# State-space stage: GpSimd takes four of sixteen C products, in-place products in a ring of four states, separate B and C rings

## The reference, cut to what matters

```python
x = einsum('ed,bld->bel', in_proj_w, ctx)            # 512 channels, 512 positions, 4 batches
u = silu(conv(x, conv_w) + conv_b)                   # 4 taps
x_dbl = einsum('ke,bel->bkl', x_proj_w, u)           # dt_lo (16), B (16), C (16)
delta = softplus(dt_proj_w @ dt_lo + dt_proj_b);  A = -exp(A_log)
def step(state, (d_t, B_t, C_t, u_t)):
    state = state * exp(d_t[..., None] * A) + (d_t * u_t)[..., None] * B_t[:, None, :]
    return state, einsum('ben,bn->be', state, C_t)
y = (ys + D * u) * silu(z)                           # z = layernorm(x)
```

## Time and profile before

| what | us |
|---|---|
| median of 3 runs | 2925.61 (2925.49 to 2928.29) |
| profiled execution, span from first to last instruction | 2923.8 |
| the runs' median over that span (what lies around it) | 1.8 |
| VectorE scans L689, 128 | 292.7 |
| VectorE products with C L698, 128 | 180.7 |
| GpSimd input products L624, 128 | 300.9 |

### The profile page before, as it was taken

How to read it: one execution, slowest core, us unless ns; L and a number is a source line. 1 busy time by engine, 2 the same in 40 slices (tenths; PEclk the granted TensorE clock), 3 DMA queues, 4 the chain that set the end, 5 groups by cost and what they waited for, 6 DMA issues and landing times. The chain is left out here.

```text
span 2923.8 us, 42347 instructions
## 1 busy us (share of the span) xinstructions
PE 2490.2 (85%) x11348; PEld 1764.4 (60%) x11366; DVE 1863.9 (64%) x3083; ACT 1281.9 (44%) x2516; POOL 1538.0 (53%) x1262
## 2 busy tenths in 40 slices
PE   5998986597218699999999983999999999999797
PEld 2333432275216577777777762778777777877553
DVE  6999999865206544664444445775776676565586
ACT  4566664242106532322222211555555555555375
POOL 2656556323660166677666726774664665444122
PEclk8999999888659899999999995999999999999999
DMA  6989898635553499998778746443543543343101
GB/s 201 291 273 295 260 294 280 209 116 222 198 198 115 178 327 321 324 318 288 256 255 267 251 140 193 156 155 124 162 154 110 174 155 119 101 130 101 58 1 58
DMA packets 271499, 572.10 MB, mean 196 GB/s; under 512 B 26992, under 2 KB 92656, under 8 KB 270592
## 3 DMA queue, kind: packets, MB, share of 16 engines
q1 hardware_dynamic: 218080, 381.54, 39.6%
q0 software_dynamic: 44032, 167.80, 17.1%
q10 hardware_dynamic: 9248, 21.11, 2.1%
HBM read 361.69 MB, written 208.67 MB: 195 GB/s over the span
## 5 line engine op out<-in xcount | busy, mean ns | idle before, releaser
L624 POOL TENSOR_TENSOR b_u<-du,bc 128x1024 f32<-128x1024 f32 x128 | 300.9, 2351 | 214.7 <-DVE c_state L698 103.7
L450 PE MATMUL ps_y<-c_state,ident 128*128 128x512 f32 x512 | 255.1, 625 | 90.2 <-DVE c_state L698 90.2
L2002 ACT ACTIVATE prob<-ps_s,neg,q_rs 128x512 f32<-128x512 f32 x256 | 196.9, 773 | 264.1 <-DVE neg L2192 256.6
L689 DVE TENSOR_TENSOR_SCAN state<-ps_decay,b_u 128x1024 f32<-128x1024 f32 x128 | 292.7, 2287 | 14.6 <-POOL b_u L624 2.3
L1519 PE MATMUL ps_o<-w_dn,hid_t 96*128 x632 | 297.8, 593 | 0.0
L1555 ACT ACTIVATE silu_g<-ps_gu 128x192 f32<-128x192 f32 x159 | 52.5, 330 | 531.5 <-PE ps_gu L1500 531.5
L2096 POOL TENSOR_SCALAR prob<-prob,rden 128x512 f32<-128x512 f32 x256 | 174.6, 691 | 199.6 <-DVE rden L2200 199.6
L1500 PE MATMUL ps_gu<-w_gu_high,rows_t_high 128*128 (+1 forms) x636 | 228.2, 359 | 12.2 <-POOL w_gu_low L1385 10.8
L450 PEld LDWEIGHTS ps_y<-c_state,ident 128*128 128x128 f32 x512 | 92.8, 194 | 234.5 <-DVE c_state L698 143.9
L1385 POOL TENSOR_TENSOR w_gu_low<-raw_gu,w_gu_high 128x1536 fp32r<-128x1536 f32 x64 | 223.5, 3492 | 11.7 <-POOL w_gu_high L1383 11.7
L522 ACT ACTIVATE ps_decay<-delta,a_neg 128x511 f32<-128x511 f32 x256 | 165.7, 681 | 140.9 <-DVE state L689 139.7
(11 more groups left out here) (349 smaller groups left out, 6054.8 us busy)
## 6 DMA issues: line engine op xcount, KB each, us to landing
bc<-bc_dram SPq DMA_DIRECT2D x128, 512.0 KB
raw_gu<-in_gate_up POOLq DMA_DIRECT2D x64, 768.0 KB, 5.7
rows<-rows_dram SPq DMA_DIRECT2D x160, 256.0 KB, 4.7
y_dram<-y SPq DMA_DIRECT2D x158, 256.0 KB, 4.5
rows_dram<-zeros SPq DMA_DIRECT2D x46, 768.0 KB
w_q<-wq_dram SPq DMA_DIRECT2D x64, 512.0 KB, 3.6
w_o<-wo_dram SPq DMA_DIRECT2D x16, 2048.0 KB
w_dn<-in_down POOLq DMA_DIRECT2D x64, 384.0 KB, 6.1
```

Source lines behind the costliest of these rows:

```text
L450: mm = pe.matmul(ps_y[e][:, :], c.ident[:, :], c_state[:, q % 2, g, :], start=False, stop=False)
L624: pool.tensor_tensor(out=b_u[:, q % 2, :, :], in0=slot(du, n).rearrange("p (a l) -> p a l", a=1).broadcast_to([P, G, SEQ]), in1=bc[:, g % ...
L689: dve.tensor_tensor_scan(state[:, q % 2, :], decay[q % 2][:, :], b_u[:, q % 2, :, :].rearrange("p g l -> p (g l)"), 0.0, ALU.mult, ALU.add ...
L2002: act.activation(prob[:, qt, :], ps_s[qt % 2][:, :], ACT.Exp, scale=q_rs[:, k % 2, qt:qt + 1], bias=neg[:, qt:qt + 1], accum_out=den[:, qt ...
```

## The change

The product with C of the steps q with q % 16 in (1, 5, 9, 13) goes from VectorE to GpSimd, which makes `help_product(q-3)` ahead of `input_product(q)`. The products, helped or not, are made in place in `state`, now a ring of four; `c_state` is gone. `b_u` is a ring of three, and the input product no longer waits for product(q-3) and waits for scan(q-3) instead of scan(q-2). B and C rows have rings and semaphores of their own (three and four groups). `load_b(g)` waits for the input products of group g-3, `load_c(g)` for the products of group g-4. TensorE adds a helped step one step later. The context has one buffer, loaded once the projections that read it are done. The two zero-filled buffers are 194 tiles, of which 194 and 66 are filled.

```diff
-FILLS, FILL, FILL_Y = BATCH * NG // 2 - 1, 14, 5
...
-        BR = 3
+        B_RING, C_RING, U_RING, S_RING = 3, 4, 3, 4
+        HELPED = (1, 5, 9, 13)
...
-        ctx_t = p.sb("ctx_t", [P, 2, KC, SEQ])
+        ctx_t = p.sb("ctx_t", [P, KC, SEQ])
...
+        def helped(q):
+            return q >= 0 and q % PAIR in HELPED
+        def by_pool(q):
+            return sum(map(helped, range(q)))
+        def by_vector(q):
+            return max(q, 0) - by_pool(q)
...
             def load_ctx(b):
+                wait(sp, x_made, b * EC)
...
-                wait(sp, product_made, 2 * (g - BR + 1))
...
+            def load_b(g):
+                wait(sp, input_made, 2 * (g - B_RING + 1))
...
+            def load_c(g):
+                wait(sp, product_made, by_vector(2 * (g - C_RING + 1)))
+                wait(sp, help_made, by_pool(2 * (g - C_RING + 1)))
...
-                load_bc(g)
+                load_b(g)
+                load_c(g)
                 if r == 4 and b + 2 < BATCH:
-                    sp.wait_ge(x_made, (b + 1) * EC)
                     load_ctx(b + 2)
...
-                for dram, skip, n in ((m.rows_dram, 0, FILLS * FILL), (m.y_dram, MINT, FILLS * FILL_Y)):
+                for dram, skip, n in ((m.rows_dram, 0, MAXT + 2), (m.y_dram, MINT, MAXT + 2 - MINT)):
...
+            def add_up(q):
+                for g in range(G):
+                    mm = pe.matmul(ps_y[q % 2][:, :], c.ident[:, :], rows_of(state, q)[:, g, :], start=False, stop=False)
+                return mm
...
-                pe.wait_ge(product_made, q + 1)
-                for g in range(G):
-                    mm = pe.matmul(ps_y[e][:, :], c.ident[:, :], c_state[:, q % 2, g, :], start=False, stop=False)
-                mm.then_inc(product_used, 1)
+                if helped(q - 1):
+                    pe.wait_ge(help_made, by_pool(q))
+                    add_up(q - 1).then_inc(help_used, 1)
+                if not helped(q):
+                    pe.wait_ge(product_made, by_vector(q + 1))
+                    add_up(q).then_inc(product_used, 1)
...
-                waits(bc_loaded[g % BR], g // BR * 32 + 32)
+                waits(b_loaded[g % B_RING], g // B_RING * 16 + 16)
                 waits(du_made, n + 1)
-                waits(scanned, q - 1)
-                waits(product_made, q - 2)
+                waits(scanned, q - U_RING + 1)
                 after_sums((q - 3) // STEPS, (q - 3) % STEPS)
...
+            def help_product(q):
+                g = group_of(q)
+                waits(c_loaded[g % C_RING], g // C_RING * 16 + 16)
+                waits(scanned, q + 1)
+                pool.tensor_tensor(out=rows_of(state, q), in0=rows_of(state, q), in1=c_row[:, g % C_RING, :, :],
+                                   op=ALU.mult).then_inc(help_made, 1)
...
             for q in range(BATCH * STEPS):
+                if helped(q - 3):
+                    help_product(q - 3)
                 input_product(q)
...
-                wait(dve, product_made, q - 1)
+                if helped(q - S_RING):
+                    dve.wait_ge(help_used, by_pool(q - S_RING + 1))
+                else:
+                    wait(dve, product_used, by_vector(q - S_RING + 1))
...
-                product(q)
+                if not helped(q):
+                    product(q)
```

More of the change, by code:

```diff
@@ L196, in state_space @@
         bn6, bn2, vare = p.sb("n0_bn6", [P, NT, 6]), p.sb("n0_bn2", [P, NT, 2]), p.sb("n0_vare", [P, NT])
-        bc = p.sb("bc", [P, BR, 2, G, SEQ])
-        b_u = p.sb("b_u", [P, 2, G, SEQ])
-        state, c_state = p.sb("state", [P, 2, G * SEQ]), p.sb("c_state", [P, 2, G, SEQ])
+        b_row, c_row = p.sb("b_row", [P, B_RING, G, SEQ]), p.sb("c_row", [P, C_RING, G, SEQ])
+        b_u = p.sb("b_u", [P, U_RING, G, SEQ])
+        state = p.sb("state", [P, S_RING, G * SEQ])
         gate, gated = p.sb("gate", [P, EC, SEQ]), p.sb("gated", [P, 2, SEQ])
@@ L206, in state_space @@
         x_loaded, small_loaded, filled = p.sem("x_loaded"), p.sem("small_loaded"), p.sem("filled")
-        ctx_loaded = [p.sem("ctx_loaded0"), p.sem("ctx_loaded1")]
+        ctx_loaded = p.sem("ctx_loaded")
         x_made, x_copied, diag_made = p.sem("x_made"), p.sem("x_copied"), p.sem("diag_made")
@@ L218, in state_space @@
         normed = p.sem("n0_made")
-        bc_loaded = [p.sem(f"bc_loaded{i}") for i in range(BR)]
+        b_loaded = [p.sem(f"b_loaded{i}") for i in range(B_RING)]
+        c_loaded = [p.sem(f"c_loaded{i}") for i in range(C_RING)]
         ready = p.sem("ssm_ready")
@@ L222, in state_space @@
         scanned, product_made, product_used = p.sem("scanned"), p.sem("product_made"), p.sem("product_used")
+        help_made, help_used = p.sem("help_made"), p.sem("help_used")
         gate_made, y_summed, y_gated = p.sem("gate_made"), p.sem("y_summed"), p.sem("y_gated")
@@ L234, in group_of, with rows_of @@
             return b * (STEPS // 2) + s // 2
+        def helped(q):
[4 more added lines that the diff above has]
+            return max(q, 0) - by_pool(q)
+        def rows_of(x, q):
+            return x[:, q % S_RING, :].rearrange("p (g l) -> p g l", g=G)
         def slot(x, n):
@@ L248, in load_ctx @@
             def load_ctx(b):
-                sp.dma_start(ctx_t[:, b % 2, :, :], d["ctx_t"][b * CD:(b + 1) * CD, :].rearrange("(k p) l -> p k l", p=P))\
-                    .then_inc(ctx_loaded[b % 2], 16)
+                wait(sp, x_made, b * EC)
+                sp.dma_start(ctx_t[:, :, :], d["ctx_t"][b * CD:(b + 1) * CD, :].rearrange("(k p) l -> p k l", p=P))\
+                    .then_inc(ctx_loaded, 16)
             def store_bc(b):
@@ L254, in store_bc, with spread_rows @@
                 sp.dma_start(m.bc_dram[b, :, :], dbc[DR:DR + 2 * DS, :]).then_inc(dbc_stored, 16)
-            def load_bc(g):
+            def spread_rows(g, n):
                 b, ng = g // (STEPS // 2), g % NG
-                wait(sp, product_made, 2 * (g - BR + 1))
[L259 to L262, removed]
+                return m.bc_dram[b:b + 1, n * DS + ng * G:n * DS + (ng + 1) * G, :]\
+                    .rearrange("a n l -> a (n l)").broadcast_to([P, G * SEQ])
+            def load_b(g):
+                wait(sp, input_made, 2 * (g - B_RING + 1))
+                sp.dma_start(b_row[:, g % B_RING, :, :].rearrange("p g l -> p (g l)"), spread_rows(g, 0))\
+                    .then_inc(b_loaded[g % B_RING], 16)
+            def load_c(g):
+                wait(sp, product_made, by_vector(2 * (g - C_RING + 1)))
+                wait(sp, help_made, by_pool(2 * (g - C_RING + 1)))
+                sp.dma_start(c_row[:, g % C_RING, :, :].rearrange("p g l -> p (g l)"), spread_rows(g, 1))\
+                    .then_inc(c_loaded[g % C_RING], 16)
             def fill(dram, first, last):
@@ L304, in project @@
             def project(b, ec, out):
-                pe.wait_ge(ctx_loaded[b % 2], b // 2 * 16 + 16)
+                pe.wait_ge(ctx_loaded, b * 16 + 16)
                 for k in range(KC):
-                    mm = pe.matmul(out[:, :], w_in[:, k, ec * P:(ec + 1) * P], ctx_t[:, b % 2, k, :],
+                    mm = pe.matmul(out[:, :], w_in[:, k, ec * P:(ec + 1) * P], ctx_t[:, k, :],
                                    start=k == 0, stop=k == KC - 1)
@@ L618, in input_product @@
                 g = group_of(q)
-                waits(bc_loaded[g % BR], g // BR * 32 + 32)
+                waits(b_loaded[g % B_RING], g // B_RING * 16 + 16)
                 waits(du_made, n + 1)
-                waits(scanned, q - 1)
-                waits(product_made, q - 2)
+                waits(scanned, q - U_RING + 1)
                 after_sums((q - 3) // STEPS, (q - 3) % STEPS)
-                pool.tensor_tensor(out=b_u[:, q % 2, :, :],
+                pool.tensor_tensor(out=b_u[:, q % U_RING, :, :],
                                    in0=slot(du, n).rearrange("p (a l) -> p a l", a=1).broadcast_to([P, G, SEQ]),
-                                   in1=bc[:, g % BR, 0, :, :], op=ALU.mult).then_inc(input_made, 1)
+                                   in1=b_row[:, g % B_RING, :, :], op=ALU.mult).then_inc(input_made, 1)
+            def help_product(q):
[4 more added lines that the diff above has]
+                                   op=ALU.mult).then_inc(help_made, 1)
             waits(n_eps, 1)
@@ L630, in _ @@
             for q in range(BATCH * STEPS):
+                if helped(q - 3):
+                    help_product(q - 3)
                 input_product(q)
+            for q in range(BATCH * STEPS - 3, BATCH * STEPS):
+                if helped(q):
+                    help_product(q)
         @block.vector
@@ L687, in scan @@
                 dve.wait_ge(input_made, q + 1)
-                wait(dve, product_made, q - 1)
-                dve.tensor_tensor_scan(state[:, q % 2, :], decay[q % 2][:, :],
-                                       b_u[:, q % 2, :, :].rearrange("p g l -> p (g l)"),
+                if helped(q - S_RING):
```

(14 more changed lines are left out.)

## The result

| what | before | after |
|---|---|---|
| median of 20 runs, us | 2925.45 (2913.85 to 2933.54) | 2935.2 (2921.41 to 2940.11) |
| profiled execution, span (time) | 2923.8 | 2924.6 (2926.1) |
| last scan of the state-space loop starts at | 553.25 | 561.64 |

The ratio after to before is 1.0031, with a 95% interval from 1.0019 to 1.0042: 9 us slower. 2946 had been forecast. The loop of the profiled execution ends 8.4 us later; its later stages are 7.6 us shorter than in the profile before, within what runs of one kernel differ by, so from here on the loop is compared and not the span.

The account below looks back on a forecast made before the run. VectorE was taken to set the 3.61 us step, its products and GpSimd's excluding one another over the SBUF port. Terms -0.4+3.9+3+11+3=+20.5 gave a span of 2944.3, forecast as 2946; own range 2932 to 2962, chance 0.50.

Parts of the forecast that it names:

- three signs that it named against itself: Wrong if: 20-step stretches below 74 us; VectorE product at full speed beside GpSimd's helped one; idle for B(5) under 3 us.
- the seam: Between two GpSimd products that follow without a gap, a waiting VectorE product was assumed to get the port.
- Rival 1: GpSimd keeps the port while its next product is ready: 2.36 more in four steps, +75 us, 3001; chance 0.18.
- The new one takes 15.02: Four steps inside a batch take 15.02 us, a 20-step stretch 75.8; all four stretches together -0.4 us.
- Rows in their own rings: GpSimd's 46.7 us of waits for B and C rows go; effect counted in the stretches' sum, DMA staying hidden.
- Batch ends: 12-step stretches over a batch's end take 52.7 us each, three against 154.2 before: +3.9 us.
- SyncE's queue: Context load in group 4 waits for the next batch's projections and delays B(5): +11 us for two batches, bounds 0 and +16.
- Store of B and C: In group 12, B(13) queues behind that wait and zero fills, U(26) 1 us late: +3 for three batches, 0 to +6.
- Four states, products in place, PE: TensorE adds a helped product one step later, but with a ring of four no scan waits: 0 us.
- First ten steps: At the loop's start the helped product of step 1 falls among VectorE's start-up products: +3 us, 0 to +6.
- Rival 2: Faster: batch ends and SyncE stall cost nothing, the port is the only bound, 3.76 a step: 2907 us; chance 0.17.
- Rival 3: No change: stall half as long (+5), batch ends and start even: 2925 to 2931 us; chance 0.15.

Follow-up runs that it names:

- own-wait run: The changed kernel with one wait put back: scan(q) waits again for the product made just before it on VectorE; one run of 2954.91 us.

## Why the prediction was wrong

It had the sign and the mechanism of the port, but forecast +20.5 for +9. That 2935.2 falls in the forecast's own range (2932 to 2962) is partly luck: a cycle walked 12.4 us too long in all is offset by batch ends walked 6.8 too short. Of the three signs that it named against itself, one came: the 20-step stretches fell below 74. By its own steps:

- *What bounds the kernel, and the port.* Right: exclusion, 1.08 behind a GpSimd product, 2.21 behind a VectorE one, the order within a cycle, the seam. Rival 1 (GpSimd keeps the port) is refuted by the cycle at 344.27. What held at 2192.35, behind a root, was not tried.
- *"The new one takes 15.02": the step that failed.* The walk put each scan 0.12 behind the product before it, as the old rows show. That gap was the scan's own wait, which the diff removes in the lines that make the ring of four; I read them as "no scan waits" for TensorE and did not see which wait they had replaced. Without it the scan starts 0.07 before the product's end: three times 0.19 in a cycle, of which 0.46 arrive, 14.56. The term for the four stretches was -0.4 and is 4x72.7-303.6=-12.8. The own-wait run gives most of it back (76.0 and 76.5 for a walk of 75.8).
- *Rows in their own rings.* Right: the waits went; with the other edits away the stretches fell by 2 to 4 us.
- *Batch ends: +3.9, measured 2.4+2.6+5.7=+10.7.* The walk was right to S(32) within 1.2 us (25.0 for 23.8), with a product held by H(29) and the input product behind it, but let TensorE add its third sum in 3.4 us. It took 6.4 after 4.7 us idle, at the lower clock. Its idle time was priced as time alone. Of the 154.2 that it was compared with, the first two ends held a part of the sum at the lower clock and the last (49.4) none; that is 1.7 of the third end's +5.7. Keeping the help out of the ends gave 2.2 to 2.5 each, keeping TensorE at work 2.5 and 2.8 in two ends and 0.6 in the third.
- *SyncE's queue: +11, measured 3.9+4.1=8.* The input product that waits for B(5) starts 16.0 and 16.2 after S(6) of its batch, for the 15 forecast; the slack that the shorter cycle has took up part of it. Batch 0 was no worse than batch 1. Moving the load gave 7.9 at these two steps.
- *Store of B and C: +3, measured 0.* No input product waits for a B row behind the store in any batch.
- *Four states, products in place, PE: 0, measured 0.8 in each of batches 0 and 1,* at step 20. "No scan waits" failed there: the scan waits for TensorE to have added the state that it overwrites. TensorE had taken 3.65 for a group of sums that took 1.98 in batch 2 after the same idle time (granted clock 0.53 from 129.3 to 132.9, and 1.00 in batch 2), and TensorE's work behind it came 1.7 later:

```profile
129.28 3.65 PE L456 MATMUL ps_y<-state,ident 128*128 128x512 f32 x4 [2.54 <-DVE state L745]
...
141.15 2.29 DVE L737 TENSOR_TENSOR_SCAN state<-ps_decay,b_u 128x1024 f32<-128x1024 f32 x1 [0.70 <-PE ps_y L456]
...
390.34 1.98 PE L456 MATMUL ps_y<-state,ident 128*128 128x512 f32 x4 [2.54 <-DVE state L745]
```

- *First ten steps: +3.* S(6) comes 1.95 late, 1.3 of it before the first scan, which started between 51.5 and 53.4 in the runs shown here; no run looked into that. The stretch itself grew by 0.6. With no help at s = 1 its third step takes 4.8 and not 5.85, so H(1) costs 1.0.
- *End of the loop:* -1.1 from the shorter cycle, which was put at 0.
- *Rival 2 (faster):* refuted for the whole, but its port floor of 15.02 a cycle was no floor, for the reason above.
- *Rival 3 (no change, 2925 to 2931):* refuted, though not by much. The ratio's interval starts at 1.0019, and 0.31% is more than the 0.2% up to which no change was to be told; its stall of 5 was 8 and its even batch ends were +10.7.

Sum: 1.95-12.8+10.7+8+1.6-1.1=8.4, the loop's measured delay.

What was bought and sold, by kernels that differ in one thing each: the help costs 24 us of loop (561.6 against 537.8; 30 with the context loaded late), the context's wait 8 to 9 with the help. Without the help, tying the scan again costs 24 (561.8 against 537.8) and tying the input product again 16 (539.1 against 522.9); freeing the scan alone, in the kernel before, gave no time. The change carried a gain and hid it under the help.

## What to carry to other kernels

Moving work from VectorE to an idle GpSimd did not pay here, because the two waited for each other over the port: add up both engines' two-input SBUF operations before counting idle time. When a ring grows, list the waits that go with it, an engine's wait for its own last instruction first, and look for a second chain of the same length before counting on one. A wait of TensorE may be paid twice, once as idle time and once at the lower clock. When stretches of one kernel differ, as 52.4 and 49.4 did here, read their granted clocks before taking either as the base of a forecast.

## What the runs showed of the hardware

- A VectorE product with two SBUF inputs that waits for the port gets it between two GpSimd products that follow each other without a gap (351.19 in the cycle shown), as in the earlier trace rows at 1800.83.
- A scan that waits for the product just before it on its own engine starts 0.20 us behind that product; without the wait it starts 0.07 before the product's recorded end.
- After 4.7 us without work TensorE ran eight passes in 6.4 us at a granted clock of 0.57, against 3.6 when extra products kept it busy. After 2.8 us without work, in the kernel before, the same sum took 5.3 in one batch end and 3.7 in another.
- A busy engine can be a waiting one: 128 equal input products took 300.9 us of GpSimd before and 360.5 after.
